# One table of expert sums in a graph and mixture-of-experts layer: every scatter-add waits for the landing of the one ahead

## The reference, cut to what matters

```python
xn = _layernorm(x, axis=-1)                       # 6250 nodes of 256 values
x = x + gnn(xn, edge_weight, src, dst) + mix(xn)  # segment sum over 100000 edges; an attention of second order
z = _layernorm(x, axis=-1)
# the part that the change is about
gate_logits = z @ gate_w + gate_b                 # 16 experts
topk_vals, topk_idx = top_k(gate_logits, 2)
topk_w = softmax(topk_vals)
h = relu(z @ w1[e] + b1[e]);  expert_out = h @ w2[e] + b2[e]
moe = sum over the 2 chosen experts of topk_w * expert_out
y = z + moe
out = x + (y - mean(y)) / sqrt(var(y) + 1e-5) * gamma + beta
```

## Time and profile before

| | us |
|---|---|
| median of 3 runs | 2509.28 (2501.57 to 2512.36) |
| profiled execution, its own time | 2514.59 |
| its span, first to last instruction | 2512.8 |
| expert loop, first to last scatter-add | 1953.8 to 2417.7 |
| loads of the sums, first issue, to the first DVE instruction of the tail | 2421.6 to 2433.2 |
| tail, from there to the end | 2433.2 to 2512.8 |

### The profile page before, as it was taken

One profiled execution on the slowest core, in us unless ns is written; L12 is line 12 of the kernel. 1 busy time (PEld: TensorE's weight loads), 2 busy tenths in 40 slices (PEclk: granted clock), 3 DMA queues, 4 the chain that ended last, 5 costly groups with the idle time before them and its releaser, 6 DMA issues.

```text
span 2512.8 us, 43084 instructions
## 1 busy us (share of the span) xinstructions
PE 1922.6 (77%) x11890; PEld 1275.7 (51%) x11938; DVE 1521.2 (61%) x3822; ACT 1094.9 (44%) x3069; POOL 1367.3 (54%) x1265
## 2 busy tenths in 40 slices
PE   4647766788889888788888888887553999999940
PEld 2435543455455555444444444444552888888830
DVE  6888888788888888444444444555444333333348
ACT  3735452333333333355554454553441444444433
POOL 1173334677777777666666665663564455433333
PEclk9669788899999999999999999998555999999975
DMA  7410001222222222233332332336553455555574
GB/s 279 134 37 26 27 25 27 81 87 86 87 89 88 86 86 85 89 91 96 97 96 89 93 97 88 99 93 101 177 190 114 88 95 95 95 95 95 95 200 155
DMA packets 160920, 248.21 MB, mean 99 GB/s; under 512 B 26161, under 2 KB 122803, under 8 KB 160756
## 3 DMA queue, kind: packets, MB, share of 16 engines
q0 software_dynamic: 64496, 144.32, 23.2%
q1 hardware_dynamic: 93300, 99.37, 13.0%
q10 hardware_dynamic: 2960, 2.57, 0.3%
HBM read 182.25 MB, written 63.91 MB: 98 GB/s over the span
## 4 chain that ended last, share of the span: by engine, by line
PE 36%; issue 7%; DVE 5%; ACT 5%; another core or an unknown queue 4%; DMA 1%; SPq 1%; DVEq 0%; POOL 0%; POOLq 0%; ACTq 0%
PE bqk L2119 9%; PE bank L2099 8%; PE b L1850 4%; PE bank L1975 3%; PE bqk L1986 3%; PE b L1864 2%; PE b L1852 2%; ACT big L935 1%; PE bank L2059 1%; ACT big L993 1%; ACT mid L993 1%; PE b L2089 1%; DVE big L1636 1%; DVE st L1160 1%
## 5 line engine op out<-in xcount | busy, mean ns | idle before, releaser
L795 POOL DMA_INDIRECT big<-xn_dram,big x832 | 858.5, 1032 | 431.0 <-issue 221.6
L1850 PE MATMUL b<-big 128*128 128x256 f32 x1468 | 411.3, 406 | 36.6 <-issue 18.0
L1402 DVE TENSOR_TENSOR acc<-acc,b 128x256 f32 x465 | 193.0, 415 | 305.0 <-PE b L1850 150.9
L1850 PEld LDWEIGHTS b<-big 128*128 128x128 f32 x1468 | 269.5, 198 | 209.8 <-issue 114.6
L824 POOL DMA_INDIRECT sum_dram<-mid,idxy x113 | 175.3, 1551 | 283.1 <-ACT mid L1067 240.5
L935 ACT ACTIVATE big<-big 128x128 f32<-128x128 f32 x832 | 265.5, 402 | 50.5 <-DVE big L1378 18.0
L2119 PE MATMUL bqk<-big,mid 128*128 x896 | 223.3, 392 | 22.6 <-issue 20.8
L2099 PEld LDWEIGHTS bank<-late,mid 128*128 128x128 f32 x1808 | 222.2, 194 | 5.9
L2099 PE MATMUL bank<-late,mid 128*128 128x128 f32 x1808 | 222.5, 277 | 0.0
L2119 PEld LDWEIGHTS bqk<-big,mid 128*128 128x128 f32 x896 | 161.3, 190 | 65.0 <-issue 47.3
L1725 DVE TENSOR_TENSOR mid<-bqk,mid 128x256 f32<-128x256 f32 x112 | 47.6, 425 | 240.4 <-PE bqk L2119 175.4
(11 more groups left out here) (336 smaller groups left out, 3484.8 us busy)
## 6 DMA issues: line engine op xcount, KB each, us to landing
big<-w SPq DMA_DIRECT2D x32, 512.0 KB
mid<-z_dram SPq DMA_DIRECT2D x114, 130.0 KB, 2.1
mid<-b SPq DMA_DIRECT2D x113, 128.0 KB
big<-xn_dram,big POOLq DMA_INDIRECT x832
sum_dram<-mid SPq DMA_DIRECT2D x19, 640.0 KB, 13.7
big<-sum_dram SPq DMA_DIRECT2D x18, 640.0 KB, 8.8
acc<-x_pad SPq DMA_DIRECT2D x10, 640.0 KB, 6.5
xn_dram<-big SPq DMA_DIRECT2D x9, 640.0 KB
```

The source lines that it names most:

```text
L795: pool.indirect_dma_start(out=gx[t % GB], out_offset=None, in_=xn_dram, in_offset=bass.IndirectOffsetOnAxis(ap=dstA[:, t:t + 1], axis=0)). ...
L1402: v.tensor_tensor(mine, mine, ps_pair[p % 2][:, C * j:C * (j + 1)], ALU.add).then_inc(s_add, 1)
L1850: a = pe.matmul(ps_pair[p % 2][:, 0:C], wd[t % (2 * EB)], gx[t % GB], start=(j == 0), stop=(j == 1))
```

## The change

`sum_dram` becomes a single table, which starts as z. Tile t's scatter-add waits for the landing of tile t - 1 instead of tile t - 2. The zeroing of the second table (ten stores of 640 KB and one of 128 KB at the start), its ten loads in the tail, and DVE's addition of the two tables go.

```diff
-        sum_dram = [nc.dram_tensor(f"sum_dram{k}", [NP + P, C], F32).ap() for k in range(2)]
+        sum_dram = nc.dram_tensor("sum_dram", [NP + P, C], F32).ap()
...
-            for a in range(0, NT, U):
-                sp.dma_start(sum_dram[1][a * P:(a + U) * P, :].rearrange("(p r) c -> p (r c)", p=P), zero).then_inc(s_zz, 16)
-            for k in range(2):
-                sp.dma_start(sum_dram[k][NP:NP + P, :], zero[:, 0:C]).then_inc(s_zz, 16)
+            sp.dma_start(sum_dram[NP:NP + P, :], zero[:, 0:C]).then_inc(s_zz, 16)
...
             for u in range(NU):
                 n = unit_tiles(u)
-                for k, a in ((0, zc[u]), (1, z1[u])):
-                    sp.dma_start(a[:, 0:n, :], sum_dram[k][u * U * P:(u * U + n) * P, :].rearrange("(u p) c -> p u c", p=P)
-                                 ).then_inc(s_zl[u // 2], 16)
+                sp.dma_start(zc[u][:, 0:n, :], sum_dram[u * U * P:(u * U + n) * P, :].rearrange("(u p) c -> p u c", p=P)
+                             ).then_inc(s_zl[u // 2], 16)
...
             for t in range(FT):
                 pool.wait_ge(f_ys, t + 1)
-                if t >= 2:
-                    pool.wait_ge(s_ysc[(t - 2) % 4], 16 * ((t - 2) // 4 + 1))
-                pool.indirect_dma_start(out=sum_dram[t % 2], in_=yo[t % 4], in_offset=None,
+                if t:
+                    pool.wait_ge(s_ysc[(t - 1) % 4], 16 * ((t - 1) // 4 + 1))
+                pool.indirect_dma_start(out=sum_dram, in_=yo[t % 4], in_offset=None,
...
             def combine_front(u):
 
                 n = unit_tiles(u)
-                v.wait_ge(s_zl[u // 2], 64)
-                link(v.tensor_tensor(zc[u][:, 0:n, :], zc[u][:, 0:n, :], z1[u][:, 0:n, :], ALU.add))
+                v.wait_ge(s_zl[u // 2], 32)
                 row_stats(lambda j: zc[u][:, j, :], u, n)
                 v.sem_inc(s_cst, 1)
```

More of the change, by code:

```diff
@@ L416, in program @@
         zc = [big[:, U * C * u:U * C * (u + 1)].rearrange("p (u c) -> p u c", u=U) for u in range(NU)]
-        z1 = [big[:, U * C * (NU + u):U * C * (NU + u + 1)].rearrange("p (u c) -> p u c", u=U) for u in range(NU)]
-        gamma_b = big[:, 2 * U * C * NU:2 * U * C * NU + C]
+        gamma_b = big[:, U * C * NU:U * C * NU + C]
         bank = [ctx.enter_context(nc.psum_tensor(f"bank{k}", [P, 512], F32)) for k in range(4)]
@@ L644, in _ @@
                 sp.wait_ge(s_z, u * U + n)
-                sp.dma_start(sum_dram[0][u * U * P:(u * U + n) * P, :].rearrange("(u p) c -> p u c", p=P),
+                sp.dma_start(sum_dram[u * U * P:(u * U + n) * P, :].rearrange("(u p) c -> p u c", p=P),
                              zt5[u % 3][:, 0:n, 0:C]).then_inc(s_zst[u % 3], 16)
@@ L1651, in _ @@
             sort_finish()
-            v.wait_ge(s_zz, 16 * (NU + 2))
+            v.wait_ge(s_zz, 16)
             v.wait_ge(s_accb, NU)
```

## The result

The changed kernel takes **2537.1 us** (median of 4, 2530.4 to 2540.1) against 2510.8 for the kernel before, measured beside it: a ratio of **1.0115, 95% interval 1.0086 to 1.0144**. It is slower, by 29 us by the ratio and 26 by the medians, where I had forecast a gain of 5.5 and given slower one chance in ten; the range ended at 2517. The profiled execution takes 2534.84.

What follows compares the result with a forecast made beforehand. The prediction took PE to set the loop's pace at 4.17 us per tile. Its terms, +3.0 - 3.4 - 1.5 - 3.6 = -5.5 us, gave 2503.8 us from 2509.3, range 2495 to 2517.

Steps and rivals of the forecast that it cites:

- The new wait in the loop: Expert loop: each scatter-add waiting for the one ahead costs 0, with 0.17 us of cover per round.
- C: Cycle of chained scatter-adds, issue to landing plus gap to POOL's next start: 4.00 us, bounds 3.61 and 4.3.
- the first rival: Expert loop: scatter-adds become the bound once the cycle reaches 4.17 us; slower by +15 or +58 us; chance 10%.
- No row before shows the gap.: Expert loop: POOL's gap behind this DMA called unseen; SP's 0.24 us after the last landing taken as nearest.
- its low bound: Stage 1's chained scatters: 2.06 us idle plus 1.55 us of generation gives 3.61 us for the cycle.
- The reading of the earlier trace: Expert loop: the landing comes within about 0.1 us of POOL's start anyway, even in a short step.
- DVE's copy: Expert loop, part of the first rival: w1's 0.69 us copy could enter the cycle, 4.69 us, +58 us.
- The drain: Last two tiles of the loop: the chain binds there, +3.0 us (from +2.2 to +3.6).
- The loads of the sums: Start of the tail: two of four loads go before DVE's first instruction, -3.4 us.
- DVE's addition in the tail: Tail: removing it saves 1.5 us for unit 0 and 3.6 us in later rounds, each 6.8 us instead of 7.2.
- The second and third rival: Tail: POOL still comes first, 2507.4 us, chance 15%; DVE's shift gets ahead of POOL, 2487 us, chance 5%.
- The start: Start of the program: dropping the zeroing gains 0; between 0 and -2 us possible.

Runs made afterwards that it cites:

- experiment 4: Changed kernel with POOL's two waits swapped (landing first, ACT's weighing second): ratio 1.0145 to the kernel before.
- experiment 6: DVE's copy of w1 written as its maximum with itself: waits swapped, ratio 1.0248; kernel before, 1.0087; changed kernel, 2363.6 us against 2323.8 before.
- experiment 7: DVE's copy of w1 cut to 8 of 512 columns: changed kernel with waits swapped, ratio 1.0131; kernel before, 2320.5 us; changed kernel, 2363.4 us.
- experiment 3: Changed kernel with the eleven zeroing stores kept, into an unread table: 2367.4 us; partner without them (changed kernel of experiment 6) 2363.6 us.
- experiment 8: Changed kernel, waits swapped: short w1 copy with full bias load, ratio 1.0093; short copy, bias to 16 partitions, 0.9924; full copy, short bias, 2515.3 us.

## Why the prediction was wrong, by its own steps

- **The new wait in the loop: the step that failed.** Forecast was C = 3.76 + 0.24 = 4.00, under the pace of 4.17, at a cost of 0. The landing was right (3.78). The gap was SP's, taken for POOL's, and its upper bound, 0.3, was also not POOL's. POOL's is 0.73 at least and 0.77 on average behind a landing when the wait for it is the second in the code, so C is 4.4 in the drain and 4.55 in the loop. The condition of the first rival, "it decides at 4.17", was right. Its sizes, +15 and +58, enclose the +43.7 of the loop without its last two steps; its second size came by another mechanism, though, and 10% was too little. With 0.17 us of cover, an error of half a microsecond in the gap decides the case.
- **"No row before shows the gap."** The trace of the kernel before does show POOL's gap, if not behind this DMA. Stage 1's scatters, which the prediction took for its low bound, have two waits as well, and the one for the landing of the scatter ahead is the second (L771). The first line is that wait, the second the start behind it:
```profile
L771 POOLq EVENT_SEMAPHORE  x1: 17/17/17, 160.7 to 160.7; - x1
```
```profile
161.46 0.97 POOL L772 DMA_INDIRECT rec_dram<-big,idxs  x1 [2.03 <-DMA rec_dram<-big,idxs]
```

The wait instruction ends at about 160.76 and the scatter starts 0.70 later. Of the 34 scatters of stage 1 that have this wait right ahead of them, 26 start 0.745 us behind the landing, seven 0.77 and one 1.13. The idle time of 2.06 in the earlier trace rows is thus some 1.3 of transfer and 0.75 of gap, and as a bound of 3.61 for C it mixed another transfer's landing with the gap that was being sought. An estimate from these rows: 3.76 + 0.75 = 4.51, and 112 x 0.34 = +38 us in the loop, where I had put 0.

- **The reading of the earlier trace rows.** I saw that the landing came at about the time of POOL's start and took it for harmless. The rows could have said more: in the kernel before POOL starts on average 0.47 us behind the landing of the tile ahead, and as close as 0.12. A gap of its own above that average must stretch the steps. What could be asked of the trace was how small the gap may be before it hurts, not that it is small.
- **DVE's copy**, named for the rival: experiments 4, 6 and 7 show that it stretches generation where the two meet. In the changed kernel as written they hardly meet. It is no part of this result.
- **The drain**: +3.0 forecast; the last two steps, 4.42 and 4.34, take 3.7 more than before. The 0.7 is the same error once more.
- **The loads of the sums**: 8.1 us from the first load to DVE's first instruction forecast, 2459.92 - 2451.98 = 7.94 measured.
- **DVE's addition in the tail**: L1630 was to start 0.30 ahead of POOL and take 1.49. It starts at 2477.72, 0.29 ahead of 2478.01, and takes 1.49. POOL does wait for DVE: 3.93 instead of 2.88. A round is 6.63, forecast 6.8. The second and third rival are out. The tail gave 10.1 against a sum of 8.5: 3.6 from the loads against 3.4, and 6.5 from DVE's first instruction on against 5.1, as the rounds are 0.2 shorter than forecast. That DVE and POOL wait for each other's whole instructions in SBUF, as weighed there, agrees with these rows.
- **The start**: 0 forecast, nothing found in experiment 3.

So the four terms of the start and the tail were right within 1.6 us together, and the two that rest on C, a borrowed number, were 44 us short. The agreement of the 4.0 of the forecast with the drain of experiment 4 (4.14 and 3.89) is luck as far as the gap goes: it holds for an order of waits that neither kernel has.

## What to carry to other kernels

Before a wait on a transfer is put into a loop, price the whole cycle on the engine that will wait: the landing and that engine's own restart. A restart read from another engine's queue is not its price; look in the same trace for a place where this engine waits in the same way. If the margin of the cycle is smaller than what is unmeasured in it, the loop is at risk whatever the central number says. Where a chain of transfers does become the bound, another transfer or a long DVE instruction that falls into it can lengthen every round (the bias load and the copy of w1 in experiment 8), though the same two did not hold up the scatter-adds of the kernel before. And look at the order of waits on one engine: it moved 0.5 us here, from the one that had an instruction of its own to the one that the scatter-add carried.

## What the runs showed of the hardware that I had not expected

- POOL's start behind the wait that ends last takes 0.73 to 0.80 us when that wait is the second in the code (an instruction of its own in the trace), and 0.27 when it is the first (carried by the scatter-add). It is so for landings and for ACT's semaphore alike. SP's takes 0.24. What POOL does in the 0.69 us behind its own wait instruction, no run tells.
- A two-input DVE instruction of 1.23 us stretches POOL's generation of descriptors from 1.55 to 2.00 on average and up to 2.6; the copy of 0.69 stretches it to 1.71 where they meet, up to 2.06.
- With the bias load cut to 16 partitions, a scatter-add of 128 rows lands 0.45 us earlier (3.79 against 4.24), though SP issues the one and POOL the other.
